# A fused attention and feed-forward block: the maxima subtracted in two halves, and the slots of the hand-written order placed anew

## The reference, cut to what matters

```python
x = x + layernorm(attn(layernorm(x)))          # LSH-weighted attention, 16 heads of 8 columns
x = x + layernorm(ffn(layernorm(x)))           # 128 -> 512 (gated) -> 512 -> 512 -> 128
# attn
scores = einsum('bhsd,bhtd->bhst', q, q) / sqrt(E)
same   = bucket[s] == bucket[t]                # 64 buckets from 6 hyperplanes
attn   = softmax(scores * (NB - 2 + same), axis=-1)
out    = einsum('bhst,bhtd->bhsd', attn, v)
# ffn
h = silu(x @ w1.T * s1) * (x @ w2.T * s2)
h = gelu(h @ h1.T * s3); h = gelu(h @ h2.T * s4); out = h @ w3.T * s5
```

## Time and profile before

| what | us |
|---|---|
| median of three runs | 1373.44 |
| the profiled execution's own time | 1380.13 |
| its span, first to last instruction | 1378.3 |
| TensorE busy (matmuls) | 1230.9 |
| VectorE busy | 1222.5 |
| GpSimd busy | 1167.3 |
| ScalarE busy | 1082.2 |
| TensorE's granted clock, mean of the span | 0.975 |

### The profile page before, as it was taken

One profiled execution on the slowest core, in us unless ns is written; L12 is line 12 of the kernel. 1 busy time (PEld: TensorE's weight loads), 2 busy tenths in 40 slices (PEclk: granted clock), 3 DMA queues, 4 the chain that ended last, 5 costly groups with the idle time before them and its releaser, 6 DMA issues. The chain is left out here.

```text
span 1378.3 us, 19705 instructions
## 1 busy us (share of the span) xinstructions
PE 1230.9 (89%) x5402; PEld 502.9 (36%) x5402; DVE 1222.5 (89%) x3838; ACT 1082.2 (79%) x1605; POOL 1167.3 (85%) x164
## 2 busy tenths in 40 slices
PE   4766799999989999998999899998989999998997
PEld 1211234334343433433343433434343343433343
DVE  4988999989999999999999999999999999999420
ACT  2344778879797988979698897979788897969875
POOL 1699889898989989899998989899898989999800
PEclk9877999999999999999999999999999999999999
DMA  4473445445544455454545535444454445543100
GB/s 105 149 186 112 118 124 147 125 122 122 143 121 129 131 136 133 116 145 120 129 115 146 134 111 139 134 129 122 128 147 119 129 122 129 136 125 100 62 5 11
DMA packets 89470, 167.37 MB, mean 121 GB/s; under 512 B 18192, under 2 KB 54160, under 8 KB 89360
## 3 DMA queue, kind: packets, MB, share of 16 engines
q1 hardware_dynamic: 89252, 165.82, 44.7%
q10 hardware_dynamic: 108, 0.30, 0.1%
HBM read 150.59 MB, written 15.47 MB: 120 GB/s over the span
## 5 line engine op out<-in xcount | busy, mean ns | idle before, releaser
L991 POOL TENSOR_TENSOR logits<-max_row,logits 128x4096 f32<-128x4096 f32 x128 | 1139.0, 8914 | 109.0 <-DMA max_row<-max_scratch 67.0
L826 DVE CUSTOM_DVE_ANT_0 logits<-s_bank,coeff 128x512 f32<-128x512 f32 x1024 | 693.6, 677 | 0.0
L1040 ACT ACTIVATE logits<-logits 128x1024 f32<-128x1024 f32 x512 | 503.0, 1046 | 81.5 <-POOL logits L991 81.2
L776 DVE TENSOR_SCALAR coeff<-brow,bcol 128x516 bf16<-128x516 bf16 x1024 | 488.1, 477 | 47.0 <-PE s_bank L560 45.1
L560 PE MATMUL s_bank<-mov_stack,stat_stack 128*128 128x512 bf16 x1024 | 348.5, 394 | 51.1 <-DVE rowmax L826 44.2
L580 PE MATMUL aux_bank<-logits,v_pad 128*32 128x512 f32 x2048 | 254.7, 617 | 34.1 <-ACT logits L1040 33.8
L715 PE MATMUL f_bank<-hid_b,h_sb 128*128 128x512 f32 x512 | 247.2, 596 | 1.3 <-ACT hid_b L1170 1.2
L704 PE MATMUL f_bank<-hid_a,h_sb 128*128 128x512 f32 x512 | 243.8, 592 | 0.0
L560 PEld LDWEIGHTS s_bank<-mov_stack,stat_stack 128*128 128x128 bf16 x1024 | 94.5, 98 | 359.1 <-DVE rowmax L826 228.0
L715 PEld LDWEIGHTS f_bank<-hid_b,h_sb 128*128 128x128 f32 x512 | 96.6, 191 | 85.6 <-issue 71.0
L704 PEld LDWEIGHTS f_bank<-hid_a,h_sb 128*128 128x128 f32 x512 | 95.0, 190 | 85.7 <-issue 77.6
(11 more groups left out here) (112 smaller groups left out, 927.7 us busy)
## 6 DMA issues: line engine op xcount, KB each, us to landing
max_row<-max_scratch SPq DMA_DIRECT2D x128, 512.0 KB, 4.1
brow<-bucket_scratch SPq DMA_DIRECT2D x63, 522.0 KB, 6.7
mov_stack<-q_scratch SPq DMA_DIRECT2D x192, 96.0 KB
stat_stack<-q_scratch SPq DMA_DIRECT2D x189, 96.0 KB
max_scratch<-rowmax_T SPq DMA_DIRECT2D x512, 1.0 KB
q_scratch<-q_parts SPq DMA_DIRECT2D x16, 384.0 KB, 4.6
x_in<-in_x SPq DMA_DIRECT2D x16, 256.0 KB, 3.1
q_scratch<-q_parts SPq DMA_DIRECT2D x16, 256.0 KB, 5.1
```

Of the source, the lines that this page charges most:

```text
L776: nc.vector.tensor_scalar(coeff[:, k % 3, :].rearrange("p (r n) -> p r n", r=ROW_RUNS), brow[:, h // 4 % 2, h % 4, :, 0:RUN], bcol[:, b % ...
L826: nc.vector.tensor_tensor_reduce(out=logits[:, ring(b, k), :], in0=tile_bank(k)[:], in1=coeff[:, k % 3, 0:SEQ], scale=float(E) ** -0.5, sc ...
L991: nc.gpsimd.tensor_tensor(tiles, max_row[:, m % 2].unsqueeze(2).broadcast_to([P, GROUP, ST, SEQ]), tiles, ALU.subtract).then_inc(below_max ...
L1040: nc.scalar.activation(logits[:, first:first + 2, :], logits[:, first:first + 2, :], ACT.Exp, scale=-1.0).then_inc(probs_done, 1)
```

## The change

It cuts the subtraction of a group in two: first the key tiles 0 and 1 of both heads, then the key tiles 2 and 3. The exponentials follow that order (the first two take tiles 0 and 1 of head one and of head two, the next two the rest). The value products of a quad wait ahead of j = 0 only for the first half of the quad's last group, and ahead of j = 2 for the rest. And nearly all slot constants have new values.

```diff
-GATE_SLOTS = (43, 45, 50, 50)
-UP_SLOTS = (47, 49, 51, 53)
-FIRST_HIDDEN_SLOTS = (56, 56, 58, 61, 62, 64, 64, 65, 65, 67, 67, 72, 73, 74, 74, 74)
-SECOND_HIDDEN_SLOTS = (77, 78, 79, 80, 80, 83, 83, 88, 88, 90, 90, 91, 92, 95, 98, 98)
-SILU_SLOTS = (44, 48)
-MULTIPLY_SLOTS = (45, 48, 52, 52)
-OUTPUT_SLOTS = (100, 103, 105, 105)
-FIRST_GELU_SLOTS = (63, 71)
-SECOND_GELU_SLOTS = (85, 96)
+GATE_SLOTS = (44, 46, 48, 48)
+UP_SLOTS = (47, 51, 52, 53)
+FIRST_HIDDEN_SLOTS = (54, 56, 58, 61, 62, 63, 63, 65, 67, 67, 67, 72, 73, 73, 74, 76)
+SECOND_HIDDEN_SLOTS = (76, 77, 78, 79, 80, 83, 83, 88, 88, 89, 91, 91, 92, 97, 98, 98)
+SILU_SLOTS = (43, 48)
+MULTIPLY_SLOTS = (45, 49, 52, 52)
+OUTPUT_SLOTS = (100, 102, 103, 105)
+FIRST_GELU_SLOTS = (65, 71)
+SECOND_GELU_SLOTS = (86, 94)
...
-COPY_LAG = 35
+COPY_LAG = 33
-DIVIDE_LAGS = (40, 40)
+DIVIDE_LAGS = (39, 39)
-X_STATS_SLOT = 4
-LATE_X_STATS_SLOT = 35
+X_STATS_SLOT = 2
+LATE_X_STATS_SLOT = 32
-LATE_X_MOMENTS_SLOT = 38
-X_PREPARE_SLOT = 23
-LATE_X_PREPARE_SLOT = 46
-X_NORM_SLOT = 50
+LATE_X_MOMENTS_SLOT = 36
+X_PREPARE_SLOT = 24
+LATE_X_PREPARE_SLOT = 36
+X_NORM_SLOT = 51
-XNT_SLOT = 58
+XNT_SLOT = 60
-Q_SLOT = 61
-Q_HIGH_SLOT = 54
+Q_SLOT = 63
+Q_HIGH_SLOT = 55
-V_SLOT = 32
+V_SLOT = 34
-Q_MIDDLE_SLOT = 58
-BCOL_SLOT = 30
-BCOL_COPY_SLOT = 27
+Q_MIDDLE_SLOT = 57
+BCOL_SLOT = 29
+BCOL_COPY_SLOT = 26
-ATT_MOMENTS_SLOT = 27
-ATT_PREPARE_SLOT = 25
-ATT_BIAS_SLOT = 28
-ATT_NORM_SLOT = 28
+ATT_MOMENTS_SLOT = 28
+ATT_PREPARE_SLOT = 28
+ATT_BIAS_SLOT = 29
+ATT_NORM_SLOT = 29
-Y1_STATS_SLOT = 33
-Y1_MOMENTS_SLOT = 34
-Y1_PREPARE_SLOT = 32
-Y1_NORM_SLOT = 34
-YNT_SLOT = 41
-YNT_COPY_SLOT = 39
-FFN_SLOT = 39
+Y1_STATS_SLOT = 34
+Y1_MOMENTS_SLOT = 36
+Y1_PREPARE_SLOT = 37
+Y1_NORM_SLOT = 37
+YNT_SLOT = 43
+YNT_COPY_SLOT = 38
+FFN_SLOT = 38
-END_PREPARE_SLOT = 53
-END_NORM_SLOT = 57
-SUB_SLOT = 14
-EXP_SLOTS = (13, 14, 14, 15)
-STORE_SLOT = 3
-LOAD_SLOT = 6
-Q_STORE_SLOT = 34
-X_LOAD_SLOT = 1
-ROW_STORE_SLOT = 46
-X_RES_SLOT = 54
+END_PREPARE_SLOT = 47
+END_NORM_SLOT = 52
+SUB_SLOT = 13
+EXP_SLOTS = (13, 13, 14, 14)
+STORE_SLOT = 4
+LOAD_SLOT = 5
+Q_STORE_SLOT = 28
+X_LOAD_SLOT = 0
+ROW_STORE_SLOT = 42
+X_RES_SLOT = 48
@@ load_maxima
-                    sp.wait_ge(below_max_done, b * GROUPS + m - 1)
+                    sp.wait_ge(below_max_done, 2 * (b * GROUPS + m - 1))
@@ weigh_values, j == 0 and then j == 2
+                    pe.wait_ge(probs_done, b * (TILES // 2) + (quad + 1) * QT // 2 - GROUP)
+                if j == 2:
                     pe.wait_ge(probs_done, b * (TILES // 2) + (quad + 1) * QT // 2)
@@ subtract
-                nc.gpsimd.tensor_tensor(tiles, max_row[:, m % 2].unsqueeze(2).broadcast_to([P, GROUP, ST, SEQ]), tiles,
-                                        ALU.subtract).then_inc(below_max_done, 1)
+                for t in (0, 2):
+                    nc.gpsimd.tensor_tensor(tiles[:, :, t:t + 2],
+                                            max_row[:, m % 2].unsqueeze(2).broadcast_to([P, GROUP, 2, SEQ]),
+                                            tiles[:, :, t:t + 2], ALU.subtract).then_inc(below_max_done, 1)
@@ exponential
-                act.wait_ge(below_max_done, b * GROUPS + m + 1)
-                first = ring(b, m * GT) + 2 * n
+                act.wait_ge(below_max_done, 2 * (b * GROUPS + m) + n // 2 + 1)
+                first = ring(b, m * GT) + ST * (n % 2) + n // 2 * 2
```

## The result

The changed kernel takes **1352.24 us** (median of four runs, 1350.88 to 1353.68), the kernel before 1374.68 beside it: a ratio of 0.9837, 95% interval 0.9817 to 0.9857. The forecast was 1357.0, in a range of 1343 to 1377, and faster. From here on lines have the numbers of the changed kernel: L560 stays, L580 is now L582 (value products), L602 L604, L676 and L690 are L678 and L692, L704 L706, L715 L717, L776 L778, L853 L855, L870 L872, L909 L911, L929 L931, L991 L994, L1010 L1014, L1040 L1044, L1053 L1057 and L1159 L1163.

A forecast was written before the change was run, and what follows sets the result against it. VectorE was the bound, busy 919.9 of 960 us. Twelve batches -8.9, two after -1.4, start -4, end -3.7 and +0.9, GpSimd +0.5 gave -16.6 us: 1357 from the median, range 1343 to 1377.

The forecast's parts named there:

- A: VectorE's stall at slot 11, behind three hidden matmuls in slot 10; spreading the hidden layers removes it, -0.74 us a batch.
- G: VectorE's stall at slot 55, behind two value parts and a hidden matmul; new in the changed kernel, not forecast.
- B: VectorE's stall at slot 21, behind the value product at slot 20; 0.89 a batch shrinks to 0.5, -0.39 us.
- C: VectorE's wait of `att_bias` for the scale on ScalarE, 0.64 a batch; half of it goes, -0.3 us.
- D: VectorE's stall at slot 44, from slots 36 to 45 with TensorE's wait for ScalarE's copy; 0.53 becomes 0.7, +0.17 us.
- E: VectorE's stall at the first multiply, with the first gate one slot later; 0.28 becomes 0.6, +0.32 us a batch.
- F: New wait of VectorE's query step, with the query product moved to slot 63; +0.2 us a batch, bounds 0 and 2.
- The end: Last value products end at 1311.6, not 1315.35: -3.7 us; gates 2 and 3 ahead of up 1 cost +0.9.
- R1: Rival: the new order only moves the stalls, leaving gains at start and end; 1367 us, chance 0.18.
- R2: Rival: ScalarE's copy ahead of the query product comes late and VectorE waits at its query step; 1385 us, chance 0.16.
- R3: Rival: the query's store, issued ahead of the maxima's load, delays that load up to 2.6 us; 1369 us, chance 0.07.
- R4: Rival: all VectorE stalls go, -40 us, 1327 with start and end; 1347 with half of them; chance 0.09.

The follow-up runs named there:

- kernel 6: kernel 1 with the hidden layers' slots and both gelus as in the changed kernel; 1361.7 us, ratio 0.989 to the kernel before.
- kernel 4: The changed kernel with the old slots of the hidden layers and their gelus; 1347.9 us, ratio 0.980 to the kernel before.
- kernel 7: kernel 1 with the new query slots and earlier copy and division of the attention output; 1356.1 us, ratio 0.986 to the kernel before.
- kernel 8: kernel 7 with the output's scaling moved ahead too (END_PREPARE_SLOT 47, END_NORM_SLOT 52); 1348.4 us, ratio 0.979 to the kernel before.
- kernel 1: The changed kernel's function bodies (the halves) with all slot constants of the kernel before; 1352.8 us, ratio 0.983 to the kernel before.
- kernel 2: All new slots, but one whole subtraction, old exponential order and one wait ahead of the value products; 1383.2 us, ratio 1.005 to the kernel before.
- kernel 11: kernel 4 with the second and third output tile one slot later; 1348.1 us, ratio 0.979 to the kernel before.
- kernel 12: kernel 11 with the first multiply one slot later, 46 for 45; 1347.4 us, ratio 0.979 to the kernel before.
- kernel 9: The changed kernel with the output's scaling back in slots 53 and 57; 1369.5 us, ratio 0.995 to the kernel before.
- kernel 10: kernel 9 with the statistics of x also back in their old slots; 1369.5 us, ratio 0.996 to the kernel before.
- kernel 5: kernel 1 with the new slots of gates, ups, silus and multiplies; 1351.3 us, ratio 0.981 to the kernel before.

## Why the prediction was right or wrong

The sign, the time (4.8 us off) and the three places of the gain were right; the inner sum was not. I had -16.6 us and the medians say -22.4; in the profiled spans the twelve batches gained 20.8 where I had 8.9. That the time still lies well inside the range is in part luck: a gain that I credited to the slots is not there, and the halves brought twice what I gave them. In the order of its steps:

- **A, -0.74: the stall went, and the gain from spreading was not there.** Two things in the change remove A, and each is enough: the spreading (kernel 6) and the end of the wait at L602 (kernels 4, 7 and 8, with the pile in place). The step that failed is the lead added up from slot 0. The count has to begin at the last place where TensorE waits for VectorE, the 0.27 at L602, which I did not have among my rows. With that wait gone the spreading has nothing left to win, and it makes G, +0.57, which the sum did not have: G goes when the old hidden slots come back (kernel 4) and comes when the new ones alone are put in (kernel 6).
- **B, -0.39: mis-sized.** I let 0.5 stand because of matmuls moved along; all 0.89 went. **C, -0.3:** all 0.64 went. B is an effect of the halves and their two waits: in kernel 1, with the old slots, it is gone. C is one of both parts: 0.23 in kernel 1, and 0.4 us in all twelve batches of kernel 2.
- **D, +0.17:** 0.53 became 0.65, as forecast in size, but it stands five slots earlier. **E, +0.32:** 0.28 became 0.33, too pessimistic. **F, +0.2:** the query step waits for nothing in the changed kernel, and 0.3 in kernel 4, inside the bounds.
- **The batch:** -0.74 - 0.89 - 0.64 + 0.12 + 0.05 + 0.57 = -1.53, against -1.73 measured and -0.74 forecast. The other 0.2 is in no wait: VectorE's busy time for a batch is 0.24 shorter (919.91 / 960 x 79.30 = 75.99, and 75.75). Why is open. (The prediction's 76.7 took the window of 960 us for twelve batches; it holds 12.1.) The profiled execution of before stands 5.5 us above its median; were these all in its batches, the batch of a median run would have gained 1.27.
- **The start, -4:** -4.8. The two stalls lost 3.3 and 2.8, at least 1.5 each as forecast.
- **The end, -3.7 + 0.9:** the value products are over 9.3 - 4.0 = 5.3 nearer to the end of the last subtraction, more than the 3.7: I had the first piece start 1.8 after that end, and it started 0.4 before it (1281.30 against 1281.68). The gates' order costs 1.26: from the first gate to the first hidden matmul it is 9.26 us (1300.62 to 1309.88) after 8.00 before (1330.29 to 1338.29). In the part called end above, kernel 1 gains 4.1 and the new slots give back 1.5. For the last two batches I had a further -1.4, which would make -4.2 with the terms above; the end as a whole lost 2.6.
- **GpSimd's second instruction, +0.18 a group:** where groups stand back to back a group takes 9.017 us from start to start against 8.883: +0.13. By the Trainium skill's 4497 ns (page "GPSIMD Engine Reference", section 3.1) it would have been 0.08; the mean in the trace is 4554 ns. It is hidden in the window, as forecast: GpSimd still idles 48.5 of 960 us, and ScalarE's waits for a subtraction (43.4 us before) are not in the list any more.
- **Rivals.** R1 (stalls only move) is near the truth for the slots, which is where I had looked for the gain (0.35 off a batch beside the halves, and nothing of the median), and wrong for the halves. R2 did not happen: no wait of the query step. R3 did not either: with the query's store ahead of the maxima's load, GpSimd's wait for the maxima is 48.3, and 49.7 in kernel 8, which has y2 early too but the load first. In the median the load lands 4.0 us after its issue and 4.1 before. The two parts of the store land after 2.9 and 3.1 us, where it was 4.6 and 5.1 behind the load, and the load, which waits for the store of the maxima first, is issued 1 to 5.5 us behind them. The 2.6 us of lateness that R3 reckoned with stands in no row. So the ring order of the page "DMA: Bandwidth & Descriptors" (Trainium skill, "Queues, rings and completion order") cost nothing that shows here. Half of R4 (1347) is what kernels 4, 8, 11 and 12 reach.

In short, the step that was mis-sized is what the halves do to a batch: I gave them -0.69 (B and C), and in kernel 1 they bring 79.30 - 77.92 = 1.38. I never priced the one line with the largest effect, the wait at j = 0, by itself.

## What to carry to other kernels

In an engine that works its queue in order, ask of each wait how much of what it waits for the next instruction really reads: cutting one wait in two, where the second half was needed two tiles later, was worth 21 us of 1374 here, with the new slots in place. Add up an engine's lead from the last place where it waited for its consumer, for anything gained ahead of that place is lost there. And move a step together with what stands behind it: the query's slots alone lost 3 us against kernel 1, with the output's scaling moved ahead of them they won 4.

## What the runs showed that was not expected

- A GpSimd subtraction of 2048 elements takes the same time beside a working VectorE (18.09 us for four at 1243.56) as in the end, where VectorE does nearly nothing (18.00 for four at 1263.68): 4.52 and 4.50.
- The program repeats itself, and yet its batches can differ: by 2.0 us before, 2.1 in kernel 7, 2.7 in kernel 9 (77.65 to 80.37), 1.5 in kernel 10 and 1.0 in kernel 2 (78.66 to 79.61); in all the others by 0.5 at most. All of the uneven ones but kernel 2 have the late y2, but so have kernels 1, 5 and 6, which are even. What makes them uneven was not tried by itself.
- In the start of the changed kernel TensorE takes 3.64 us for 16 instructions of the value product at 83.71, with its granted clock at the lower level, and 1.92 for the next 16 at 87.82, with the clock at the upper one. The granted clock of the first 100 us and of the next 80 is 0.88 and 0.85, and was 0.85 and 0.83 before, so a little of the start's gain may be the clock's; the two stalls named above lost 6.1 us together, more than the 4.8 that the start gained in all.
